# Causal attention in front of a small transformer: all scores of a pair in one group right behind the heads' products, second row block in the two banks of the projections, query product and values in banks of their own

## The reference

```
q, k, v = x @ Wq, x @ Wk, x @ Wv            # split into 16 heads of 64
logits  = (q @ k.T + causal + bias(i - j)) / 64
probs   = softmax(logits)
out     = concat(probs @ v) @ Wo + bo
```

## Time and profile before

| | |
|---|---|
| median of three runs | 2810.12 (2809.82 to 2812.38) |
| the profiled execution: time | 2812.22 |
| the profiled execution: span | 2810.4 |
| PE busy | 2649.9 (94% of the span) |
| ACT busy | 2099.4 (75%) |
| DVE busy | 2130.8 (76%) |
| POOL busy | 1629.5 (58%) |
| granted TensorE clock, mean | 0.980 |

### The profile page before, as it was taken

One profiled execution on the slowest core, in us unless ns is written; L12 is line 12 of the kernel. 1 busy time (PEld: TensorE's weight loads), 2 busy tenths in 40 slices (PEclk: granted clock), 3 DMA queues, 4 the chain that ended last, 5 costly groups with the idle time before them and its releaser, 6 DMA issues. The chain is left out here.

```text
span 2810.4 us, 71245 instructions
## 1 busy us (share of the span) xinstructions
PE 2649.9 (94%) x24208; PEld 1999.9 (71%) x24208; DVE 2130.8 (76%) x5775; ACT 2099.4 (75%) x6207; POOL 1629.5 (58%) x1947
## 2 busy tenths in 40 slices
PE   7999999999999999999959999999797999999796
PEld 4666666666666666666638888887675888888575
DVE  5677777677776777767749999998567999999665
ACT  6777777777777777777729999999346999999642
POOL 4343434343444444334349999998226999999521
PEclk9999999999999999999979999999998999999898
DMA  2000000000000000000041111111111111111112
GB/s 70 7 7 9 9 5 7 7 9 9 5 9 5 9 9 5 9 5 5 5 112 39 40 40 40 39 39 38 45 29 35 40 39 41 40 41 39 45 34 77
DMA packets 128513, 77.07 MB, mean 27 GB/s; under 512 B 80196, under 2 KB 110736, under 8 KB 128144
## 3 DMA queue, kind: packets, MB, share of 16 engines
q1 hardware_dynamic: 127968, 72.34, 10.4%
q10 hardware_dynamic: 176, 0.07, 0.0%
HBM read 17.58 MB, written 8.41 MB: 9 GB/s over the span
## 5 line engine op out<-in xcount | busy, mean ns | idle before, releaser
L301 POOL TENSOR_SCALAR L<-L,rinv 128x128 f32<-128x128 f32 (+3 forms) x1024 | 522.7, 532 | 701.1 <-DVE rinv L482 701.1
L364 ACT ACTIVATE L<-L,nmax 128x128 f32<-128x128 f32 (+3 forms) x1024 | 565.1, 556 | 10.0 <-DVE nmax L469 1.2
L469 DVE CUSTOM_DVE_ANT_0 L<-bank,bias_tab 128x128 f32<-128x128 f32 (+3 forms) x1024 | 473.7, 486 | 95.9 <-PE bank L584 89.8
L876 ACT ACTIVATE f_L<-bank,f_nmax,f_rn 128x128 f32<-128x128 f32 x1024 | 459.8, 485 | 6.0 <-DVE f_nmax L1003 6.0
L853 POOL TENSOR_TENSOR f_rn<-f_ssq,f_mhalf 128x16 f32<-128x16 f32 x128 | 419.0, 3273 | 18.2 <-DVE f_ssq L987 4.6
L835 POOL TENSOR_TENSOR f_qkr<-f_ab 128x256 f32<-128x256 f32 x512 | 414.2, 837 | 11.3 <-DVE f_ab L954 11.3
L954 DVE TENSOR_TENSOR f_ab<-bank,f_tab 128x512 f32<-128x512 f32 x512 | 348.1, 680 | 8.3 <-ACT f_sq L866 8.3
L605 PE MATMUL bank<-ident,L 128*128 128x128 f32 x2560 | 351.0, 276 | 1.0 <-DVE PT L210 1.0
L605 PEld LDWEIGHTS bank<-ident,L 128*128 128x128 f32 x2560 | 289.3, 141 | 40.2 <-DVE PT L210 6.7
L210 DVE COPY PT<-bank 128x512 f32<-128x512 f32 x384 | 264.8, 690 | 51.9 <-PE bank L605 50.8
L623 PE MATMUL bank<-PT,v 128*64 128x512 f32 (+3 forms) x2048 | 303.9, 439 | 0.0
(11 more groups left out here) (145 smaller groups left out, 6409.6 us busy)
## 6 DMA issues: line engine op xcount, KB each, us to landing
f_vm<-f_v SPq DMA_DIRECT2D x224, 128.0 KB, 2.4
f_hs<-xf SPq DMA_DIRECT2D x132, 32.0 KB
f_hs<-xf SPq DMA_DIRECT2D x132, 31.8 KB
xb<-in_L_attn_x SPq DMA_DIRECT2D x16, 256.0 KB, 2.9
out<-yacc SPq DMA_DIRECT2D x32, 128.0 KB, 1.8
f_hs<-xf SPq DMA_DIRECT2D x32, 128.0 KB
out<-f_acc SPq DMA_DIRECT2D x4, 1024.0 KB, 7.5
f_hs<-xf SPq DMA_DIRECT2D x32, 127.0 KB
```

The source lines that it names most:

```text
L301: nc.gpsimd.tensor_scalar(t, t, rinv[:, h % RING, a, i:i + 1], 1.0, ALU.mult, ALU.mult).then_inc(s_N, 1)
L364: nc.scalar.activation(t, t, ACT.Exp, bias=nmax[:, p % RING, a, i:i + 1], scale=-1.0, accum_out=rsum[:, p % RING, a, i:i + 1]).then_inc(s_ ...
L469: nc.vector.tensor_tensor_reduce(out=L[:, p % RING, a, LOFF[i]:LOFF[i] + (i + 1) * P], in0=ps_s[a][i % 2][:, 0:(i + 1) * P], in1=bias_tab[ ...
L876: nc.scalar.activation(L[:, ot % 2, a, k, :], ps_s[a][:, k * P:k * P + P], ACT.Exp, bias=nmax[:, ot % 2, a, k:k + 1], scale=rn[:, ot % 2, ...
```

## The change

- The order of PE's slot becomes: scores(0), (2), (1), (3), transposes(0), query product, transposes(1), (2), values, transposes(3), in p=4 x's transposes, y, transposes(4), key product, heads out. The next slot's scores stand right behind heads out.
- Banks: block 0 and block 2 of head a lie side by side in bank 2a, block 3 in bank 2a+1, block 1 in 256 columns of `ps_o` (head 0) or `ps_item` (head 1). The query product and y move from `ps_item` to `ps_o`; key product, values and x's transposes stay in `ps_item`.
- So scores(1) wait until o of the tail before is copied out, scores(0) until seven of the eight logits of the pair before are taken, scores(3) until all are; the query product waits for logits (1,0), the values for logits (1,1), heads out for the y addition.
- DVE and ACT take the blocks in the order of `TAKEN`; ACT's exponential (3,1) goes into the next slot.
- Fill 4 goes from DVE to ACT (`COPIER` is `DADAA`).
- The value blocks are made one slot later (two of them ahead of the first slot, not three); the bias table's products use two banks, not three.

The diff, without the hunks on the table and the first values (`range(3)` becomes `range(2)`, `n % 3` becomes `n % 2`):

```diff
...
 LAG = 2
-COPIER = "DADAD"
+COPIER = "DADAA"
+TAKEN = ((1, 0), (1, 1), (0, 1), (2, 1), (2, 0), (3, 0), (0, 0), (3, 1))
 def at(b, per, k):
...
 def value_item(b, p, par):
-    if p >= 5:
-        return (b + 1, p - 5, 1 - par) if has_scores(b) and has_next(b) else None
-    return (b, p + 3, par) if has_scores(b) else None
+    if p >= 6:
+        return (b + 1, p - 6, 1 - par) if has_scores(b) and has_next(b) else None
+    return (b, p + 2, par) if has_scores(b) else None
 def y_step(b, p, par):
...
     return (b - 1, p + 4, 1 - par)
+def taken(b, p, i, a):
+    return at(b, 8 * HP, 8 * p + TAKEN.index((i, a)) + 1)
 def copies(b, p, engine, upto):
...
         flip = o[:, 0, 0:P]
-        ps_s = (bank[0:2], bank[2:4])
         ps_t, ps_o, ps_item = bank[4:6], bank[6], bank[7]
-        ps_q0, ps_k0, ps_v0, ps_flip = bank[0], bank[1], (bank[2], bank[3], bank[7]), bank[4:7]
+        ps_s = [(bank[2 * a][:, 0:P], (ps_o, ps_item)[a][:, 0:2 * P], bank[2 * a][:, P:T], bank[2 * a + 1][:]) for a in range(2)]
+        ps_q0, ps_k0, ps_v0, ps_flip = bank[0], bank[1], bank[2:4], bank[4:6]
         s_x = [sem("x_loaded_even"), sem("x_loaded_odd")]
...
                         copy_fill(act, nc.scalar.activation, "A", tail, k, (ACT.Copy,))
-                def exps(i, a):
-                    if not has_scores(b):
+                def exps(i, a, pair=(b, p)):
+                    if pair is None or not has_scores(pair[0]):
                         return
-                    act.wait_ge(s_L, at(b, 8 * HP, 8 * p + 2 * i + a + 1))
-                    t = L[:, p % RING, a, LOFF[i]:LOFF[i] + (i + 1) * P]
-                    nc.scalar.activation(t, t, ACT.Exp, bias=nmax[:, p % RING, a, i:i + 1], scale=-1.0,
-                                         accum_out=rsum[:, p % RING, a, i:i + 1]).then_inc(s_E, 1)
-                first = isinstance(b, int) and b == 0 and p < 2
+                    eb, ep = pair[:2]
+                    act.wait_ge(s_L, taken(eb, ep, i, a))
+                    t = L[:, ep % RING, a, LOFF[i]:LOFF[i] + (i + 1) * P]
+                    nc.scalar.activation(t, t, ACT.Exp, bias=nmax[:, ep % RING, a, i:i + 1], scale=-1.0,
+                                         accum_out=rsum[:, ep % RING, a, i:i + 1]).then_inc(s_E, 1)
+                first = b == 0 and p < 2
+                exps(3, 1, lagging(b, p, par, 1))
...
+                exps(1, 1)
+                if lead is not None:
+                    high(lead, s_q, q_hi, s_qh, ps_o)
                 fills(1)
-                exps(0, 0)
-                if lead is not None:
-                    high(lead, s_q, q_hi, s_qh)
+                exps(2, 1)
+                if item is not None:
+                    value_out(item)
                 exps(0, 1)
-                exps(1, 0)
...
                 fills(3)
-                exps(1, 1)
+                if p == 4 and has_scores(b) and has_next(b):
+                    xT_high(b + 1, 1 - par)
                 exps(2, 0)
-                if COPIER[4] == "A":
-                    fills(4)
+                fills(4)
+                exps(0, 0)
                 if lead is not None:
                     high(lead, s_k, k_hi, s_kh)
-                exps(2, 1)
                 exps(3, 0)
-                exps(3, 1)
+                exps(1, 0)
                 if tail is not None:
...
                     nc.scalar.activation(o[:, h % 4, :], ps_o[:], ACT.Copy).then_inc(s_O, 1)
-                if item is not None:
-                    value_out(item)
-                if p == 4 and has_scores(b) and has_next(b):
-                    xT_high(b + 1, 1 - par)
             pair_slots(act, slot, 4)
...
                 def logits(i, a):
                     if not has_scores(b):
                         return
-                    dve.wait_ge(s_S[a], at(b, 4 * HP, 4 * p + i + 1))
-                    if i == 0:
+                    dve.wait_ge(s_S[a], at(b, 4 * HP, 4 * p + (2, 3, 2, 4)[i]))
+                    if (i, a) == TAKEN[0]:
                         dve.wait_ge(s_T, at(b, 5 * HP, 5 * (p - RING + 1)))
-                        if isinstance(b, int) and b == 0:
+                        if b == 0:
                             dve.wait_ge(s_far, p + 1)
...
                     nc.vector.tensor_tensor_reduce(
-                        out=L[:, p % RING, a, LOFF[i]:LOFF[i] + (i + 1) * P], in0=ps_s[a][i % 2][:, 0:(i + 1) * P],
+                        out=L[:, p % RING, a, LOFF[i]:LOFF[i] + (i + 1) * P], in0=ps_s[a][i],
                         in1=bias_tab[:, 2 * p + a, T - (i + 1) * P:T], scale=-1.0 / DH, scalar=3.0e38,
...
                         copy_fill(dve, nc.vector.tensor_copy, "D", tail, k)
+                logits(1, 0)
                 before = lagging(b, p, par, 1)
...
                                          rsum[:, h % RING].rearrange("p a i -> p (a i)")).then_inc(s_R, 1)
-                logits(0, 0)
+                logits(1, 1)
+                fills(0)
                 logits(0, 1)
-                fills(0)
-                logits(1, 0)
-                logits(1, 1)
+                logits(2, 1)
+                if lead is not None:
+                    low(lead, s_qh, q_hi, q_lo, s_ql, ps_o)
                 fills(2)
-                if lead is not None:
-                    low(lead, s_qh, q_hi, q_lo, s_ql)
                 logits(2, 0)
-                logits(2, 1)
+                logits(3, 0)
                 if step is not None:
...
                     src = xb[:, ypar, half, :] if j < 2 else yacc[:, half, :]
-                    nc.vector.tensor_tensor(yacc[:, half, :], ps_item[:, 0:2 * D].rearrange("p (t d) -> p t d", d=D), src,
+                    nc.vector.tensor_tensor(yacc[:, half, :], ps_o[:, 0:2 * D].rearrange("p (t d) -> p t d", d=D), src,
                                             ALU.add).then_inc(s_Ya, 1)
-                logits(3, 0)
-                if COPIER[4] == "D":
-                    fills(4)
+                if p == 4 and has_scores(b) and has_next(b):
+                    xT_low(b + 1, 1 - par)
+                logits(0, 0)
                 if lead is not None:
                     low(lead, s_kh, k_hi, k_lo, s_kl)
                 logits(3, 1)
-                if p == 4 and has_scores(b) and has_next(b):
-                    xT_low(b + 1, 1 - par)
                 if p == 2 and has_scores(b) and has_next(b):
...
                 if p == 3 and has_scores(b) and has_next(b):
...
                         pe.wait_ge(s_kl, at(b, HP, p + 1))
-                    pe.wait_ge(s_L, at(b, 8 * HP, 8 * p + 2 * i - 2))
+                        pe.wait_ge(s_L, at(b, 8 * HP, 8 * p - 1))
+                    elif i == 1:
+                        pe.wait_ge(s_O, at(b, HP, p - 2))
+                    elif i == 3:
+                        pe.wait_ge(s_L, at(b, 8 * HP, 8 * p))
                     r, tok, keys = p % 2, slice(i * P, i * P + P), slice(0, (i + 1) * P)
...
                             row = slice(DH * a, DH * a + DH)
-                            last[a] = nc.tensor.matmul(ps_s[a][i % 2][:, keys], qq[row, r, tok], kk[row, r, keys],
+                            last[a] = nc.tensor.matmul(ps_s[a][i], qq[row, r, tok], kk[row, r, keys],
                                                        start=(n == 0), stop=(n == 2))
...
                         pe.wait_ge(s_Ve, at(hb, HP, 4 if h == 0 else 8))
-                    pe.wait_ge(s_O, at(hb, HP, h))
+                    if step is not None:
+                        pe.wait_ge(s_Ya, at(step[0], HP, step[1] + 1))
+                    else:
+                        pe.wait_ge(s_ql, at(b, HP, p + 2))
                     for step_, (j, places) in enumerate(((0, ((0, 0), (1, 0))), (1, ((2, 0), (3, 0))),
...
                         pe.wait_ge(s_wo, 16)
-                    pe.wait_ge(s_O, at(yb, HP, 2 * g + 2))
+                    pe.wait_ge(s_O, min(at(b, HP, p - 2), HP * B))
+                    if lead is not None:
+                        pe.wait_ge(s_ql, at(b, HP, p + 2))
+                    elif has_scores(b):
+                        pe.wait_ge(s_L, taken(b, p, 1, 0))
+                    else:
+                        pe.wait_ge(s_Ya, at(b, HP, p - 4))
                     for u in range(2):
...
                             pr = 2 * g + w
-                            last = nc.tensor.matmul(ps_item[:, u * D:u * D + D], o[:, pr % 4, t * P:t * P + P], wo[:, pr, :],
+                            last = nc.tensor.matmul(ps_o[:, u * D:u * D + D], o[:, pr % 4, t * P:t * P + P], wo[:, pr, :],
                                                     start=(w == 0), stop=(w == 1))
                     last.then_inc(s_Y, 1)
-                first = isinstance(b, int) and b == 0 and p < 2
-                if isinstance(b, int) and (b, p) == (0, 0):
-                    pe.wait_ge(s_Ve, 3)
+                if (b, p) == (0, 0):
+                    pe.wait_ge(s_Ve, 2)
                 scores(0)
+                scores(2)
                 scores(1)
```

(51 more changed lines are left out.)

## The result

The changed kernel took 2706.15 (median of 4 runs, 2703.72 to 2709.66), the kernel before 2810.13 beside it: ratio 0.9633, 95% interval 0.9621 to 0.9645, so 104 less. Forecast were 2694, 116 less, in a range of 2674 to 2755. Lines are those of the changed kernel's trace (span 2705.2) unless said otherwise.

A forecast was written before the change was run, and what follows sets the result against it. PE's instruction order bounds the kernel: cutting its lost time from 1.45 to 0.45 makes a slot 9.67, not 10.67 us. With all terms, 2812.2 - 116.7 = 2695.5 profiled, 2694 beside the median; range 2674 to 2755.

The forecast's parts named there:

- three seams: PE's tiling changes (full-array to or from half-array products) at transposes-scores, scores-y, heads out-values vanish: 0.08+0.11, 0.09+0.11, 0.10+0.11 us.
- the y wait: Key product behind transposes(4) waits for DVE's y addition to empty the shared bank; 0.35 us a slot would go.
- Rival 2: Time at tiling changes belongs to each product group's start, so only the 0.35 y wait goes: 2767 us; chance 0.07.
- p=4: Slot with x's transposes, where the key product waits for xT_lo: 1.84 us above an ordinary slot, against 1.41 before.
- the seam within the score group: On PE, 256-wide scores right behind 128-wide ones lost 0.05 us a slot; counted as gone.
- PE is fed: ACT, DVE and POOL deliver in time for PE's denser order, so nothing new waits and the slot is 9.67 us.
- the walk: Every engine's instructions timed through one ordinary slot from its first score matmul; tightest spare 0.07 us, k_lo's 0.5.
- Rival 1: ACT's bank-emptying copies bound the slot: 0.33 us longer, 2736 us in all; chance 0.21 together with Rival 4.
- the first batch: Batch taking 87.91 us before: two slow table-building slots unchanged give or take 3, two without y at 9.35; 4 less.
- Rival 3: Keys (k_hi, k_lo) late under heads out, so next scores wait: 1.8 late gives 2850 us; chance of slower 0.07.
- the tail: End of the kernel: the last batch's last slot and the four slots after it, together 0.5 us less.
- Rival 4: Pauses in p=4 lower PE's granted clock, costing some 3 us a batch: 2740 us; chance 0.21 together with Rival 1.

The follow-up runs named there:

- run 2: The kernel before with only y moved to the bank of heads out, so the key product no longer waits for the y addition: 2769.6 us, ratio 0.9853.
- run 1: The changed kernel with scores(3) behind transposes(0), adding two changes between half-row and full-array products: 2757.81 us, ratio 0.9813.
- run 4: The changed kernel with fill 4 moved back from ACT to DVE, behind logits (0,0): 2702.91 us, ratio 0.962.
- run 9: The changed kernel with ACT's k_hi placed behind exponentials (3,0) and (1,0): 2793.11 us, ratio 0.9939.
- run 8: The changed kernel with fill 2 also moved from DVE to ACT, ahead of the value copy: 2724.44 us, ratio 0.9693.
- run 3: The changed kernel with score blocks in the order 0, 1, 2, 3, leaving only block 0 ahead of block 1: 2769.37 us, ratio 0.9855.
- Run 5: The changed kernel with DVE's xT_lo ahead of the y addition in p=4: 2695.35 us, ratio 0.9598.

## Why the prediction was right, step by step

- *A slot is the sum of PE's starts; three seams and the y wait go.* Right. Slot 9.72 for 9.67; run 2 prices the wait at 0.33 (0.35 forecast), run 1 a seam at 0.20 (0.19 to 0.21 forecast for those that went). Rival 2, that seams are no drains, fell with run 1. From half columns to half rows, the boundary that no row of before had, the cost is 0.10 on the last matmul of heads out (0.32 to its successor, where the one of the same width before it took 0.22) and 0.05 on the first of the scores. The Trainium skill (TensorEngine Tiling (Array Packing), Key Properties) says that a change of tiling mode drains TensorE. The trace agrees for this boundary too, as far as a cost can show a drain.
- *The y wait: the sum right, its parts not.* The prediction split the 0.35 into 0.24 of waiting and 0.11 of a slow first matmul, and took both as gone. The first matmul stays slow, 0.32 (750.15 to 750.47); what went is 0.33 ahead of it (0.68 to 0.35), so the last transposes overlap their successor more than the 0.11 each of the prediction allows. The same holds for the 0.11 in its sum of p=4. The totals came out although the split was wrong.
- *Mis-sized: the seam within the score group.* The 0.05 that the 256-wide block cost behind the 128-wide ones was taken as gone. It came back with the 384-wide block (744.00 to 744.23). The fourteen middle batches, 106.1 forecast and 99.8 measured, miss by 6.3, and 0.05 x 112 slots are 5.6 of it.
- *PE is fed.* Right in an ordinary slot, to 0.06 at each point of the walk. Rival 1, ACT as the bound: not so there (run 4), but so in slots 2 and 3 of the first batch. Rival 3: the keys have 0.45 to spare (run 9). A longer queue on ACT eats into both links, o and the keys, and has 0.38 (run 8); rival 1 priced only the first. The wait on o, priced at nothing for its cover, costs 0.52 with less of it (run 3; 0.8 was the forecast with none). The walk's "want ps_o at 0.80" does not fit its own cover of 0.91; scores(1) start at 0.97.
- *p=4.* Right: 1.84. Run 5 confirms the cause, the order of y addition and xT_lo on DVE.
- *Mis-sized: the first batch, 3.5 of the missing.* It was to be 4 shorter and is 0.5 shorter. I gave slots 2 and 3, without y, 9.35. Slot 3 took 9.42. Slot 2 took 12.04 because it started at the low clock: 0.75 over the slot (0.50 from 44.02 to 50.03, which is the lower of its two levels, 1.2 GHz, and 1.00 behind), after a pause of 2.63 at the end of slot 1. Before, this slot took less, at 0.86:

```profile
43.45:54.24 10.79, 10.79 (x70) 7.68 (x69) 8.03 (x29) 7.80 (x24) 5.51 (x11) 0.86 0.00 0
```

  Slots 0 and 1 were 0.6 and 0.8 longer than before, in their 3. In both, the key product now stands 1.07 for the copy of the values, which share its bank and have moved ahead of it. The 4 was itself too small: slots 2 and 3 took 10.79 and 9.36 before, so 9.35 for each and the walk for the other four make the batch 5.1 shorter. Without that slip the miss would be 4.5.
- *Mis-sized: the tail.* 1.1 longer and not 0.5 shorter. The step that the prediction left out is the move of ACT's exponential (3,1) into the next slot. In the first slot behind the last scores it stands behind the copy of o, the reciprocal of the sums waits for it, and in DVE's queue fill 0 waits behind the reciprocal. So PE waits 1.28 for the fill where it waited 0.35 (1405.53 before), and this slot takes 7.19 (1297.92 to 1305.11) and not 6.10 (1404.09 to 1410.19). The changed kernel, then before:

```profile
1299.44 0.20 DVE L488 RECIPROCAL rinv<-rsum 128x8 f32<-128x8 f32 x1 [3.06 <-ACT L L370]
...
1300.30 1.10 PE L611 MATMUL bank<-ident,L 128*128 128x128 f32 x8 [1.28 <-DVE PT L215]
```

```profile
1404.57 0.20 DVE L482 RECIPROCAL rinv<-rsum 128x8 f32<-128x8 f32 x1 [0.88 <-ACT L L364]
```

  The trace shows this; no run tests it.
- *Rival 4, the clock in p=4*: no; p=4 runs at 1.00 with its pauses of 0.25 and 0.68.

The misses, 6.3 + 3.5 + 1.6 and 0.4 in the last batch, less 0.2 that the time ahead of the first scores gave beyond its 0.7, make 11.6; between 116.7 and 105.2 lie 11.5. The first batch and the tail were not walked, and they hold almost half.

## What to carry to other kernels

Where PE is recorded busy throughout, read its starts and not its busy time: the spacing of neighbours shows what each change between half-array and full-array products costs, and grouping products of one tiling is then worth that price times the changes saved, so long as each copy that frees a bank still ends before its next writer. Walk one period of every engine's queue from measured starts before the edit; here the walk held to 0.06, while the terms not walked (first slots, tail) carried almost half of the error. Ask of a delay how many links it reaches: in run 8 two gave way together, and the forecast had named one. When an instruction moves into the next slot, walk the slots where the pipeline runs empty too. In an in-order queue ask of each wait what stands behind it: putting xT_lo ahead of an addition that waits for PE took 0.59 off each of fifteen slots.

## What the runs showed of the hardware

- A wider score matmul right behind 128-wide ones on the same tiling costs 0.05 to 0.06 once: 0.23 for a 384-wide one (744.00 to 744.23), where the next took 0.18, and in the kernel before 0.17 for a 256-wide one, where the next took 0.12:

```profile
802.29 0.33 PE L584 MATMUL bank<-k_hi,q_hi 64*128 64x256 f32 x2
802.46 0.28 PE L584 MATMUL bank<-k_lo,q_hi 64*128 64x256 f32 x2
```

- What a pause costs in clock differs between executions of the same order. Runs 4, 5 and 8 do not touch the first two slots, which have no fills: slot 0 took 11.13 to 11.17 in the changed kernel and in all three, slot 1 13.92 in the changed kernel's profile and 12.68, 13.69 and 12.61 in theirs (granted clock 0.75 in the first, 0.87 in run 4). The low clock stood behind pauses of 2.63; behind the 0.7 ahead of the scores in the slots of run 9 the clock stayed at 1.00.
